# Attention layer of a graph network: recurrence factors, exponentials and edge networks kept in PSUM, products in row order

## The reference

```python
h_keys, h_queries, h_values = (grouped_lin(xh, w) for w in (k_w, q_w, v_w))   # per node, 4 heads x 16
W_k = lin(ssp(lin(edge_attr, wkn_w1, wkn_b1)), wkn_w2, wkn_b2)                # per edge, 32 -> 16 -> 16
keys_j = lin(W_k[:, None, :] * h_keys[col], wkl_w, wkl_b)
qk_ij = jnp.sum(h_queries[row] * keys_j, axis=-1)
alpha = segment_softmax(qk_ij, row, n)
W_v = lin(ssp(lin(edge_attr, wvn_w1, wvn_b1)), wvn_w2, wvn_b2)
msg_j = alpha[:, :, None] * lin(W_v[:, None, :] * h_values[col], wvl_w, wvl_b)
aggr = jax.ops.segment_sum(msg_j, row, num_segments=n).reshape(n, H)
```

## Time and profile before

| | us |
|---|---|
| median of 3 runs | 7819.6 |
| lowest and highest | 7811.6, 7821.93 |
| span of the profiled execution, first to last instruction | 6240.3 |
| DVE busy in the span | 4084.2 |
| POOL busy in the span | 4166.8 |
| ACT busy in the span | 2268.7 |
| PE busy in the span | 2457.8 |

### The profile page before, as it was taken

How to read it: one execution, slowest core, us unless ns; L and a number is a source line. 1 busy time by engine, 2 the same in 40 slices (tenths; PEclk the granted TensorE clock), 3 DMA queues, 4 the chain that set the end, 5 groups by cost and what they waited for, 6 DMA issues and landing times. The chain is left out here.

```text
span 6240.3 us, 79656 instructions
## 1 busy us (share of the span) xinstructions
PE 2457.8 (39%) x26472; PEld 2145.9 (34%) x26472; DVE 4084.2 (65%) x6681; ACT 2268.7 (36%) x3099; POOL 4166.8 (67%) x3385
## 2 busy tenths in 40 slices
PE   2877666666666660000632222222222222222215
PEld 2876666666666660000421111111111111111115
DVE  6987777777777773999345655655655655655654
ACT  0033333333333332666244344344344344344332
POOL 0067777777777775000568888888888888888863
PEclk9987777777777775555555555555555555555555
DMA  4022222222222222777133233233233233233211
GB/s 57 18 79 83 74 84 74 84 80 77 83 74 84 74 81 98 271 269 256 39 97 92 81 85 91 80 85 90 80 85 91 80 86 90 80 87 89 80 54 22
DMA packets 459619, 572.09 MB, mean 92 GB/s; under 512 B 349939, under 2 KB 358003, under 8 KB 451632
## 3 DMA queue, kind: packets, MB, share of 16 engines
q1 hardware_dynamic: 309440, 265.27, 15.5%
q0 software_dynamic: 107904, 193.55, 10.9%
q10 hardware_dynamic: 42224, 112.63, 4.7%
HBM read 308.06 MB, written 263.14 MB: 92 GB/s over the span
## 5 line engine op out<-in xcount | busy, mean ns | idle before, releaser
L1126 POOL DMA_INDIRECT got_a<-kv_table,idx_a x1612 | 2390.6, 1483 | 501.1 <-issue 491.0
L497 POOL DMA_INDIRECT records<-rec,place x1612 | 1620.6, 1005 | 824.9 <-issue 491.2
L1254 DVE TENSOR_TENSOR prod<-got_a,query 128x1664 f32<-128x1664 f32 x62 | 188.8, 3046 | 1123.9 <-DMA got_a<-kv_table,idx_a 1123.9
L1140 PE MATMUL p_a<-ident,flat_attr 128*128 128x128 f32 x434 | 108.0, 426 | 1778.2 <-ACT flat_attr L1174 1778.2
L1140 PEld LDWEIGHTS p_a<-ident,flat_attr 128*128 128x128 f32 x434 | 83.5, 221 | 1790.6 <-ACT flat_attr L1174 1790.6
L518 PE MATMUL p_look<-parts,lo_hot_t 128*128 128x98 bf16 x4836 | 503.8, 240 | 129.9 <-DVE earlier L703 129.8
L609 ACT COPY lo_hot_t<-p_t 128x512 bf16<-128x512 bf16 x434 | 241.1, 556 | 711.6 <-PE p_t L542 700.2
L703 DVE TENSOR_TENSOR earlier<-p_same,less_b 128x512 bf16<-128x512 f32 x434 | 282.4, 651 | 274.7 <-PE p_same L564 269.6
L685 DVE TENSOR_SCALAR dst_hot<-p_dst,number 128x512 bf16<-128x512 f32 x434 | 309.0, 712 | 215.1 <-PE p_dst L552 213.8
L518 PEld LDWEIGHTS p_look<-parts,lo_hot_t 128*128 128x128 bf16 x4836 | 397.8, 116 | 140.6 <-DVE earlier L703 140.5
L1198 ACT COPY packed_a<-state_a 128x1768 f32<-128x1768 f32 x62 | 228.0, 3678 | 534.7 <-DVE state_a L1286 534.7
(11 more groups left out here) (307 smaller groups left out, 8628.9 us busy)
## 6 DMA issues: line engine op xcount, KB each, us to landing
rec_r<-records SPq DMA_DIRECT2D x62, 1300.0 KB, 6.5
sums<-packed_a ACTq DMA_DIRECT2D x62, 936.0 KB, 3.7
q_starts<-zero_q SPq DMA_DIRECT2D x62, 884.0 KB
qin<-q_starts SPq DMA_DIRECT2D x62, 884.0 KB, 6.9
sums<-packed_r ACTq DMA_DIRECT2D x62, 832.0 KB, 6.6
records<-rec,place POOLq DMA_INDIRECT x1612
attr_a<-records SPq DMA_DIRECT2D x62, 416.0 KB, 5.0
got_a<-kv_table,idx_a POOLq DMA_INDIRECT x1612, 2.6
```

Source lines behind the costliest of these rows:

```text
L497: nc.gpsimd.indirect_dma_start(k.records, bass.IndirectOffsetOnAxis(ap=place[b][:, t:t + 1], axis=0), rec[b][:, t, :], None).then_inc(s_se ...
L1126: nc.gpsimd.indirect_dma_start(got[b][:, t, :], None, k.kv_table, bass.IndirectOffsetOnAxis(ap=idx[b][:, t:t + 1], axis=0)).then_inc(s_got ...
```

## The change

- PSUM is divided anew: one bank each for `p_a` and `p_z`, two joined banks for `p_w`, four joined banks `wide`. `wide` holds `factor` (68 x 27 values, in the place of `keep` and `scale` both) and `weight` (4 x 26, a second copy of the exponentials of `below`). `keep`, `scale` and `net` are gone from SBUF.
- The query scan reads the marks from `factor` and writes its result over them; `prod` and the logit sum read the queries there. Later in the same turn ACT writes the decay factors into `factor`, and the state scan reads them there. As `factor` is single, ACT writes the marks of chunk n+1 (`marks`) only after the state scan of chunk n, ahead of the copy to `packed`; DVE waits for that before the query scan.
- `prod` is laid out in row order. Its first product reads `got` in order and the queries with a stride; the second and the value product read the edge networks directly in `p_w`; the sum over 16 components reads in order.
- The bias of the edge networks comes by a one-row matmul (ones times `b2_row`) that opens each accumulation in `p_w`; the two DVE additions (1245) are gone. PE may fill `p_w` anew only after the value product (`s_value`).
- The transposes and `p_z` go through their one bank in two halves with waits between PE and ACT. DVE waits for all exponentials before line 1277, where it waited for the first before.

```diff
-        keep = [tile(f"keep_a{b}", [P, QW, T1]) for b in range(2)]
-        prod = tile("prod", [P, D, T])
+        prod = tile("prod", [P, T, D])
-        scale = tile("scale", [P, QW, T1])
-        net = [tile(f"net{b}", [P, TP, EC]) for b in range(2)]
+        b2_row = tile("b2_row", [1, TP, EC])
-        p_a, p_z, p_w = ([bank(f"{n}{j}") for j in range(2)] for n in ("p_a", "p_z", "p_w"))
+        p_a, p_z = bank("p_a"), bank("p_z")
+        p_w = banks("p_w", 2)
+        wide = banks("wide", 4)
+        flat = wide[:, 0:QW * T1]
+        factor = flat.rearrange("p (c t) -> p c t", t=T1)
+        weight = wide[:, QW * T1:QW * T1 + NH * T].rearrange("p (h t) -> p h t", t=T)
...
+                        for j, (c0, c1, groups) in enumerate(halves):
+                            wait(pe, s_at_copied, 2 * n + j)
+                            for g in range(c0 // P, c0 // P + groups):
+                                last = nc.tensor.transpose(p_a[:, g * P - c0:(g + 1) * P - c0], flat_attr[:, g * G:(g + 1) * G, :].rearrange("p t c -> p (t c)"), k.ident[:])
+                            last.then_inc(s_at, 1)
+                        for j, (c0, c1, groups) in enumerate(halves):
+                            pe.wait_ge(s_at_copied, 2 * n + j + 1)
+                            wait(pe, s_z_read, 2 * n + j)
+                            nc.tensor.matmul(p_z[:, 0:c1 - c0], k.w1_t[:], attr_t[:, c0:c1], start=True, stop=True).then_inc(s_z, 1)
                         pe.wait_ge(s_soft, n + 1)
-                        wait(pe, s_net, n)
...
+                        wait(pe, s_value, n)
+                        for j, (c0, c1, groups) in enumerate(halves):
+                            nc.tensor.matmul(p_w[:, c0:c1], k.ones[0:1, :], b2_row[:, c0 // EC:c1 // EC, :].rearrange("p t o -> p (t o)"), start=True, stop=False)
...
                 def lay_out(n, i, b):
-                    wait(act, s_state, n - 1)
-                    nc.scalar.copy(keep[b][:, :, 1:T1], bc(k.same[:, cols], 1, QW)).then_inc(s_keep, 1)
...
+                def marks(n, i, b):
                     cols = bass.ds(i * 2 * T + b * T, T)
+                    nc.scalar.copy(factor[:, :, 1:T1], bc(k.same[:, cols], 1, QW)).then_inc(s_keep, 1)
...
                     act.wait_ge(s_below, n + 1)
-                    nc.scalar.activation(add[:, D:QW, 1:T1], below[:], ACT.Exp).then_inc(s_exp, 1)
-                    nc.scalar.activation(scale[:, 0:D, :].rearrange("p (h d) t -> p h d t", h=NH), bc(drop[:], 2, HD), ACT.Exp)
-                    nc.scalar.activation(scale[:, D:QW, :], drop[:], ACT.Exp).then_inc(s_exp, 1)
+                    nc.scalar.activation(add[:, D:QW, 1:T1], below[:], ACT.Exp)
+                    nc.scalar.activation(weight, below[:], ACT.Exp)
+                    nc.scalar.activation(factor[:, 0:D, :].rearrange("p (h d) t -> p h d t", h=NH), bc(drop[:], 2, HD), ACT.Exp)
+                    nc.scalar.activation(factor[:, D:QW, :], drop[:], ACT.Exp).then_inc(s_exp, 1)
...
                     act.wait_ge(s_state, n + 1)
+                    if not at_end(i, b):
+                        marks(n + 1, i + b, 1 - b)
                     nc.scalar.copy(packed[b][:, :, 0:QW], state[b][:, :, 1:T1].rearrange("p c t -> p t c")).then_inc(s_packed, 1)
...
                     dve.wait_ge(s_query, n + 1)
+                    dve.wait_ge(s_keep, n + 1)
-                    nc.vector.tensor_tensor_scan(flat, keep[b][:].rearrange("p c t -> p (c t)"), flat, 0.0, ALU.mult, ALU.add).then_inc(s_q, 1)
+                    nc.vector.tensor_tensor_scan(flat, flat, query[b][:].rearrange("p c t -> p (c t)"), 0.0, ALU.mult, ALU.add).then_inc(s_q, 1)
...
+                    c.then(nc.vector.tensor_copy(query[1 - b][:, :, 0:1], factor[:, :, T:T1]))
                     dve.wait_ge(s_w, n + 1)
-                    for j, (c0, c1, groups) in enumerate(halves):
-                        c.mark(nc.vector.tensor_tensor(
-                            net[b][:, c0 // EC:c1 // EC, :], p_w[j][:, 0:c1 - c0].rearrange("p (t o) -> p t o", o=EC),
-                            bc(k.b2_r[:], 1, G * groups), ALU.add))
...
-                    c.then(nc.vector.tensor_tensor(prod[:], got[b][:, :, 0:D].rearrange("p t c -> p c t"), query[b][:, 0:D, 1:T1], ALU.mult))
-                    c.then(nc.vector.tensor_tensor(by_head, by_head, bc(net[b][:, 0:T, 0:HD].rearrange("p t o -> p o t"), 1, NH), ALU.mult))
-                    c.then(nc.vector.tensor_reduce(logit[:], prod[:].rearrange("p (h d) t -> p h t d", h=NH), AX.X, ALU.add))
...
+                    c.then(nc.vector.tensor_tensor(prod[:], got[b][:, :, 0:D], factor[:, 0:D, 1:T1].rearrange("p c t -> p t c"), ALU.mult))
+                    by_head = prod[:].rearrange("p t (h d) -> p t h d", h=NH)
+                    nets = p_w[:, 0:T * EC].rearrange("p (t o) -> p t o", o=EC)
+                    c.then(nc.vector.tensor_tensor(by_head, by_head, bc(nets[:, :, 0:HD], 2, NH), ALU.mult))
+                    c.then(nc.vector.tensor_reduce(logit[:].rearrange("p h t -> p t h"), by_head, AX.X, ALU.add))
...
+                    value = got[b][:, :, D:2 * D]
+                    by_head = value.rearrange("p t (h d) -> p t h d", h=NH)
+                    nc.vector.tensor_tensor(by_head, by_head, bc(nets[:, :, HD:EC], 2, NH), ALU.mult).then_inc(s_value, 1)
+                    dve.wait_ge(s_exp, n + 1)
                     dve.wait_ge(s_value, n + 1)
+                    nc.vector.tensor_tensor(add[:, 0:D, 1:T1].rearrange("p (h d) t -> p h d t", h=NH), value.rearrange("p t (h d) -> p h d t", h=NH),
+                                            bc(weight, 2, HD), ALU.mult).then_inc(s_used, 1)
...
+                    nc.vector.tensor_tensor_scan(state[b][:].rearrange("p c t -> p (c t)"), flat,
                                                  add[:].rearrange("p c t -> p (c t)"), 0.0, ALU.mult, ALU.add).then_inc(s_state, 1)
```

More of the change, by code:

```diff
@@ L1204, in _ @@
                 c.begin(0)
+                marks(0, 0, 0)
                 lay_out(0, 0, 0)
@@ L1261, in chunk @@
                         c.mark(nc.vector.tensor_copy(logit1[:, :, 0:1], top[1 - b][:, :, T:T1]))
-                    c.then(nc.vector.tensor_tensor(logit1[:, :, 1:T1], logit[:], query[b][:, D:QW, 1:T1], ALU.add))
+                    c.then(nc.vector.tensor_tensor(logit1[:, :, 1:T1], logit[:], factor[:, D:QW, 1:T1], ALU.add))
                     wait(dve, s_packed, n - 1)
```

71 lines of the change are left out of this document (25 added, 46 removed).

## The result

The changed kernel took 7875.5 us (median of 4 runs, 7873.5 to 7876.5) beside 7820.8 us of the kernel before (4 runs, 7811.6 to 7825.8) on the same chip: a ratio of 1.0071, 95% interval 1.0057 to 1.0086. The forecast was 6999. The change made the kernel slower by 55 us where 820 us of gain were expected.

A forecast was written before the change was run, and what follows sets the result against it. POOL's stretched gathers bound the old loop at 46.64 us a chunk, ACT and DVE the new at 33.3; sixty-one rounds save 820 us, span 6240.3 to 5420, and 7819.6 - 820 = 6999 us, range 6925 to 7110.

The forecast's parts named there:

- 1579.3: Time outside the recorded span: the median 7819.6 us lies 1579.3 above the span 6240.3, taken as constant under the change.
- Sixty-one rounds of 33.3: Attention loop: state scans 33.3 us apart, the last starting at 5245 where it was 6065.9, 820 us less.
- F: Rival on the whole time: what lies outside the span shrinks with it, giving 6792 us; chance 0.08.
- (a): POOL's gathers in the attention loop: six long DVE instructions stop stretching them, so a chunk costs 32.5 us, from 46.5.
- Rival C: Attention loop: PSUM inputs don't free POOL, gathers stay stretched, a chunk takes 44.5 us, time 7692 us; chance 0.04.
- (b): DVE's own work: second product, sum and value product 1.89 us each, gain 4.3; first product 3.05, scans 3.98.
- (c): ACT-DVE chain tied by single `factor`: a round of 33.3 us, 0.8 above POOL's 32.5, with +0.3 for split banks.
- (d): DVE in the new round: ready 16.8 us after the last scan, ACT at 26.1, so DVE has 9 us slack.
- (e): PE's one-row matmuls into `p_w` and `p_z`: 3 to 4 us more a chunk, hidden with 4 us to spare.
- (f): ACT writing PSUM: no change taken, upper bound +4.0 us; marks and exponentials already go at 0.83 ns an element.
- Rival E: ACT's writes to PSUM cost their upper bound: 37.3 us a round, 7243 us; half of it, 7121; chance 0.10.
- Rival D: DVE slow on PSUM where it strides or writes in place, becoming the bound: round 51.0 us, time 8088; chance 0.03.

## Why the prediction was wrong, step by step

The forecast added two terms: a span of 5420, and 1579.3 for the rest of the time ("The median lies 1579.3 above the span; I take that as constant."). On a chip like the one that the profile came from the first term was right: a span of 5404.9. The second was no time outside the span. In each profiled execution since, the time lies about 2 us above the span (6246.0 and 6244.0 for before on chip 12). The 1579.3 us are what a chip with stops adds inside it.

Outside the attention loop this addition is nearly the same for both kernels, 1643 us before and 1619 changed by the table, so the constant held there, by luck and not by its reason. The term that failed is the loop's: "Sixty-one rounds of 33.3", with nothing put down for what a chip with stops makes of them. On the chip of the measurement the rounds are 33.1 and 61.6 us in turn, 46.9 on average: the loop took 2863.7 us where 61 x 33.3 = 2031, and these 832 us are nearly the whole of the 876 by which the time was missed. The overlap that the sum took for granted, of 26 gathers each 1.25 us apart with PE's work, exists on a chip without stops; on the other, PE's signals come some 28 us late in every second round. What remains, 44 us, is not placed, as before has no profile on that chip. A fifth of the time was in no view, and one rival (F, 0.08) stood for all that could be in it.

The rest, on chip 12 unless another is named:
- (a) POOL: forecast 32.5 us a chunk, gathers at 0.95. Measured 948 ns, maximum 1059 (4692 before); the run without the logarithm shows the floor at 32.48. Right. Rival C is out.
- (b) DVE: 3 x 1.89 right to 0.01. The first product was taken at the upper bound of 3.05 and costs 1.888, the lower one; the row I had called nearest misled. It cost the forecast nothing, since DVE had slack. Scans 3.98 and 3.99: right.
- (c) The round: 33.3 forecast, 33.04 measured. Right; the split banks cost nothing that shows: ACT waits for PE at four places for 5.4 us a chunk, where it waited at two for 5.3.
- (d) DVE waits 9.3 us for the exponentials, forecast 9, and 1.3 us for the marks, forecast 1.5. Right. POOL's wait for the index copy: 51.1 / 62 = 0.8 us, as forecast.
- (e) PE's one-row matmuls are hidden on a chip without stops; DVE never waits for `p_w` there. The slack was counted, but not that PE's whole chain lost POOL's cover. The runs with PE made late show what that is worth: 0 to the old loop, 11.0 us a chunk to the new. It is a risk of the change, but not the cause of the miss.
- (f) The pace of 0.83 ns an element does not follow from the row given with it (1.67 us for 1768 is 0.94). ACT's writes to PSUM: 1636 ns for the marks where the SBUF write took 1.67 us, a gain of 0.03 us each. The Trainium skill (ScalarE: Activation LUTs, Step-by-step: what each stage is for) has the sign right; the size changes nothing here. Rival E is out.
- Rival D, the only slower one, had the wrong mechanism: DVE is nowhere slow on PSUM. The slower case was real, but came by way of PE.

What stays open is what on those chips ties PE to POOL's indirect DMAs. Shown are:
- the place: PE gives out products 0.70 us apart in the sort, and ACT gets its signal 29 us late in the loop;
- the partner: with half the gathers left out the stops in the loop are gone, while 96 updates more from SyncE and another layout of PE's program change nothing;
- the end: ACT is let go between 1 us before and 9 us after the start of the run's last gather.

Whether pace, length of the run, the mean rate or the bytes decide was not told apart. The runs with stops have 52 gathers at 1.25 and 1.33 us, the run without has 13 at 1.25 us, and the old loop has all 26 a chunk at a mean of 1.79 us with signals that are late by a few us only. A rival that no run tests is the recording itself: each time given here, but those of before on the chip of the measurement, comes with the span of its own trace, and on the chip of the measurement the trace holds 2.8 semaphore updates a us in the changed loop, where by chip 12's count 10.6 took place. Whether these chips are as slow without a trace is not on record.

## What to carry to other kernels

Before a sum is made on a profile, its own span and the times must be laid side by side; a gap of a fifth is not a constant but an unread part of the kernel, and the forecast must either explain it or carry a broad case for it. Moving one of two SBUF inputs of a long VectorE instruction to PSUM frees GpSimd's DMA issue entirely (1.483 to 0.948 us a gather here). A loop whose slowest engine is made faster loses the cover it gave to all others: list each signal that was late behind it, PE's included, and ask what it costs when it comes late (0 before, 11.0 us a chunk after, for the same delay of PE). And a gain in one engine's issue rate is measured on more than one chip before it is believed: the same kernel was 13% faster here and 0.7% slower there.

## What the runs showed of the chip that I had not expected

- On the chip of the first measurement and on four of the seven numbered ones PE or its signals stand still beside runs of indirect DMAs, and the same program takes 1575 to 1625 us longer there (before) or 2470 to 2510 us (changed).
- A strided operand cost VectorE nothing when it was in PSUM and its partner and output were in order (1.888 us for 1664 elements, 1.887 all in order); strided in SBUF the same product took 3.05 to 3.44 us.
- A memset on POOL behind a gather fills part of the 0.30 us gap between two gathers: 0.22 us of work lengthened the pace by 0.08 us.
